# Routing in three groups of batches, with nine expert tiles run inside the first part

## What is computed

```python
x = x + xattn(_layernorm(x), fside, ctx)    # per batch: smooth_quant_linear, silu(gate) * up, smooth_quant_linear
t = _layernorm(x)
scores = einsum('btd,de->bte', t, router_w)                  # 8 experts
w, idx = top_k(softmax(scores), 2); w = w / sum(w)
y = sum over the two chosen e of  w_e * ((silu(t @ gate_proj[e]) * (t @ up_proj[e])) @ down_proj[e])
x = x + y
```

## Time and profile before

| | |
|---|---|
| median of 3 runs | 421.02 us (420.9 to 422.14) |
| the profiled execution | 421.27 us, span 419.4 us |
| PE, DVE, ACT, POOL busy | 77%, 50%, 50%, 59% of the span |
| first part | 0 to about 196 us |
| routing, to the first gather | about 196 to 220 us |
| 39 tiles, from the first expert matmul | 226 us to the end |

### The profile page before, as it was taken

The page is one execution under the profiler, slowest core; times in us unless marked ns, Lnnn a source line. Parts: engine busy times, 40 slices in busy tenths (PEclk is TensorE's granted clock), DMA queues, the critical chain, the costliest instruction groups (busy, mean ns, idle before and its releaser), DMA issues.

```text
span 419.4 us, 5809 instructions
## 1 busy us (share of the span) xinstructions
PE 322.5 (77%) x1712; PEld 202.4 (48%) x1738; DVE 209.2 (50%) x442; ACT 209.7 (50%) x378; POOL 246.4 (59%) x260
## 2 busy tenths in 40 slices
PE   0638758879887678861166999999999999999960
PEld 0525445567656446651143555555555555555530
DVE  2584899887898855500871333333333333323310
ACT  1558559878779767453101444444444444444430
POOL 2484698677869565458304265666566656656440
PEclk9957966995899795865555999999999999999996
DMA  7936406693178347035004266766666666675552
GB/s 258 314 115 216 161 41 203 192 358 100 26 253 325 109 144 275 27 125 225 1 0 127 36 117 102 131 112 115 120 125 106 116 110 125 106 134 102 90 70 27
DMA packets 26667, 57.00 MB, mean 136 GB/s; under 512 B 2576, under 2 KB 12816, under 8 KB 24592
## 3 DMA queue, kind: packets, MB, share of 16 engines
q0 software_dynamic: 8816, 20.71, 27.5%
q1 hardware_dynamic: 17824, 35.93, 24.6%
HBM read 37.50 MB, written 19.14 MB: 135 GB/s over the span
## 4 chain that ended last, share of the span: by engine, by line
issue 27%; POOL 12%; PE 8%; POOLq 2%; DMA 1%; ACT 0%; DVE 0%; SPq 0%
POOL xg L772 8%; PE bank_r L1007 4%; PE bank_h L1029 3%; POOLq L778 2%; POOL out L782 1%; DMA xg<-tokens,gather_at 1%; POOL hold_p L198 1%; POOL number L754 1%; PE bank_t L995 1%; PE bank_q L1018 0%; POOL out L757 0%; ACT y L953 0%; DVE aT L900 0%; ACT aT L948 0%; POOL no_later L764 0%
## 5 line engine op out<-in xcount | busy, mean ns | idle before, releaser
L1007 PE MATMUL bank_r<-gu_hi,xT 128*128 x312 | 107.0, 385 | 1.0 <-DVE xT L891 0.2
L782 POOL DMA_INDIRECT out<-y,scatter_at x39 | 61.7, 1583 | 51.2 <-ACT y L953 50.0
L891 DVE SCALAR_TENSOR_TENSOR xT<-bank_t,xT 128x512 f16<-128x512 f32 x39 | 27.0, 691 | 66.3 <-ACT xT L933 66.3
L772 POOL DMA_INDIRECT xg<-tokens,gather_at x39 | 38.5, 986 | 29.1 <-DVE gather_at L881 17.3
L1007 PE MATMUL bank_r<-gu_lo,xT 128*128 x144 | 55.1, 383 | 0.0
L1029 PE MATMUL bank_h<-dn_hi,aT 128*128 x156 | 52.8, 379 | 1.7 <-DVE aT L900 1.4
L953 ACT ACTIVATE y<-bank_h,slot_weight 128x512 f32<-128x512 f32 x39 | 26.8, 687 | 36.8 <-PE bank_h L1029 36.8
L1007 PEld LDWEIGHTS bank_r<-gu_hi,xT 128*128 128x128 f16 x312 | 30.8, 99 | 29.5 <-issue 2.5
L360 POOL TENSOR_TENSOR gu_lo<-stage,gu_hi 128x1024 bf16<-128x1024 f32 x16 | 34.0, 2129 | 13.1 <-ACT gu_hi L578 13.0
L933 ACT ACTIVATE xT<-bank_t 128x512 f16<-128x512 f32 x39 | 23.0, 589 | 24.8 <-PE bank_t L995 24.7
L906 DVE SCALAR_TENSOR_TENSOR gated<-bank_r,gated 128x256 f32<-128x256 f32 x39 | 16.6, 425 | 37.3 <-ACT gated L941 37.3
(11 more groups left out here) (156 smaller groups left out, 629.7 us busy)
## 6 DMA issues: line engine op xcount, KB each, us to landing
x_in<-in_x SPq DMA_DIRECT2D x4, 1024.0 KB, 5.4
w_in<-in_fside_BxS2xS SPq DMA_DIRECT2D x4, 1024.0 KB, 6.3
stage<-in_L_ffn_gate_proj SPq DMA_DIRECT2D x8, 512.0 KB, 4.9
stage<-in_L_ffn_up_proj SPq DMA_DIRECT2D x8, 512.0 KB, 3.7
stage<-in_L_ffn_down_proj SPq DMA_DIRECT2D x8, 512.0 KB, 4.8
x<-in_x SPq DMA_DIRECT2D x4, 1024.0 KB, 6.2
out<-x SPq DMA_DIRECT2D x4, 1024.0 KB, 6.7
tokens<-xn SPq DMA_DIRECT2D x4, 1024.0 KB, 6.4
```

The costliest lines, as they stand in the source:

```text
L772: pool.indirect_dma_start(out=xg[:, i % XG], out_offset=None, in_=tokens_dram, in_offset=bass.IndirectOffsetOnAxis(ap=gather_at[:, i:i + 1 ...
L782: pool.indirect_dma_start(out=out, out_offset=bass.IndirectOffsetOnAxis(ap=scatter_at[:, i:i + 1], axis=0), in_=y[:, i], in_offset=None, c ...
L891: dve.scalar_tensor_tensor(out=xT[i % 2][:, 1].rearrange("p c t -> p (c t)"), in0=bank_x[:, i % 2], scalar=X_SCALE, in1=xT[i % 2][:, 0].re ...
L1007: ins = pe.matmul(bank_gu[:, i % 2], xT[i % 2][:, part, c], rhs[:, cols], start=(c == 0 and n == 0), stop=(c == C - 1 and n == 2))
```

## The change

What it does:

- The batches are routed in three groups, (0, 1), (2) and (3). An expert has 16 fixed slots of 128 rows. "choose g" finds the two experts of each row, "place g" the slot and lane, with a one-hot over slots and one over lanes for each batch and choice; "table g" adds the sorted rows to a table; "list" and "indices" take the filled slots out of it as tiles.
- After group 0 the first nine (`EARLY`) full tiles are listed, gathered and run as phase 0, woven into the orders of the first part; the other 30 follow as phase 1, when group 2 is placed. There is no second block.
- The router multiplies x1, the rows ahead of the second layer norm, with weights whose column mean is taken off (`rwc`). The weights of the two choices come from the difference of their scores times `rstd`, by Tanh ("weigh g"); the softmax goes.
- The early tiles use buffers of the first part: xg and y are three rows each in the staging buffer, so all 24 pieces must be split before the first gather. `y` of the late tiles is a ring of eight.
- An early scatter waits for the landing of the one before it. ACT's "take y i" of an early tile waits until scatter i - 3 has landed.
- "x scales" and "w1 scales" make the scale of all four row groups at once, and all orders are new.
- At the start, SP waits for a memset on POOL and stores the padding rows before it loads x.

```diff
+EARLY = 9
-    "load x 0, load w1 0, load expert 0, load expert 1, load expert 2, load w2 0, load x 1, load expert 3, "
+    "load x 0, load w1 0, load expert 0, load w2 0, load expert 1, load x 1, load expert 2, load expert 3, "
...
+    GROUPS = [(0, 1), (2,), (3,)]
+    PHASES = ([(0, 0, EARLY, GROUPS[0])] if EARLY else []) + [(len(GROUPS) - 1, EARLY, MOST, range(B))]
...
+        ahead = pool_order.index(("gather", EARLY)) + 1
+        pool_order[ahead:ahead] = [("gather", EARLY + n) for n in range(1, J)]
+        act_order.append(("x high", EARLY))
+        dve_order.append(("x low", EARLY))
+        for i in range(EARLY, TILES):
+            if i + J < TILES:
+                pool_order.append(("gather", i + J))
+            pool_order.append(("scatter", i))
...
+            sp.wait_ge(sem("zeroed"), 1)
+            sp.dma_start(tokens_dram[N:N + P], blank).then_inc(sem("pad_stored"), 16)
...
+            def gather(i):
+                phase = phase_of[i]
+                if phase not in started:
+                    started.append(phase)
+                    pool.wait_ge(sem("pad_stored"), 16)
+                    pool.wait_ge(sem("lo_done"), 3 * E)
+                    for b in PHASES[phase][3]:
+                        pool.wait_ge(sem(f"tokens_stored{b}"), 16)
+                    pool.wait_ge(sem("gather_ready"), phase + 1)
+                before = before_in(3, J, i)
+                if before is not None:
+                    ring_t.done(pool, "x low", 0, before)
...
+            def scatter(i):
...
+                if i < EARLY:
+                    if i > 0:
+                        pool.wait_ge(sem("added"), 16 * i)
+                    landing = sem("added")
+                else:
+                    before = pool.value_load(scatter_after[0:1, i:i + 1], min_val=1, max_val=MOST)
+                    pool.wait_ge(sem("landed"), before)
...
+                for n, b in enumerate(GROUPS[g]):
+                    for k in range(K):
...
+                        for s in range(2):
+                            then(dve.tensor_tensor(onehot[:, k, s], number[:], spread(place_of[:, s, n, k], [P, P, J], 1), ALU.is_equal))
...
+                        if step > 0:
+                            after_sort(step - 1)
+                        dve.tensor_tensor(packed[:], spread(onehot[:, k, 0], [P, 3, P, J], 1), spread(values[:, :, b, k], [P, 3, P, J], 2),
+                                          ALU.mult).then_inc(sem("packed"), 1)
...
+            def take_y(i):
...
+                before = before_in(3, 2 * J, i)
+                if before is not None:
+                    if i < EARLY:
+                        act.wait_ge(sem("added"), 16 * (before + 1))
+                    else:
+                        act.wait_ge(sem("landed"), before - EARLY + 2)
```

More of the change, by code:

```diff
@@ new lines, in block_kernel @@
+        ring_w = Ring(pe_order, [bank_r[:, 1]], sem("w_row_filled"), sem("w_row_taken"),
+                      {"rows 1": 1, "rows 2": 1, "w1 scale row": 1, "table": 1, "indices": 1}, [("a low", 1)])
+        ring_q = Ring(pe_order, banks(bank_q), sem("q_filled"), sem("q_taken"),
+                      {"x transposed": C, "w1 transposed": C, "a transposed": IC, "w2 transposed": IC,
+                       "tokens": 2, "scores": 1, "take y": 1})
+        ring_h = Ring(pe_order, banks(bank_h), sem("h_filled"), sem("h_taken"), {"product 1": J, "product 2": J, "up first": 1})
@@ L517, in _ @@
+            in_turn(dve_order,
+                    {"choose": choose, "place": place, "table": add_to_table, "list": list_tiles, **({"done": tiles_done} if EARLY else {}),
+                     "indices": indices, "x low": x_low, "up": up, "a low": a_low,
+                     "moments 1": partial(moments, 0, x_in, sem("x_in"), 1), "moments 2": partial(moments, 1, x1, sem("x1_ready"), J),
                      "w1 columns": partial(weight_columns, "w1 columns", 0), "w2 columns": partial(weight_columns, "w2 columns", 1),
@@ L584, in silu, with take_tokens @@
                     act.activation(h[:, j:j + 2, 0:I], h[:, j:j + 2, 0:I], ACT.Silu).then_inc(sem("silu_done"), 1)
[L586 to L589 removed]
+            def take_tokens(pair):
                 for j in range(2):
[L591 to L592 removed]
@@ new lines, in sort @@
+            def sort(g):
+                bank = ring_w.fill(pe, "table", 0, g)
+                steps = K * len(GROUPS[g])
+                for n in range(steps):
+                    step = K * GROUPS[g][0] + n
+                    pe.wait_ge(sem("packed"), step + 1)
+                    for j in range(J):
+                        ins = pe.matmul(bank[:, 0:3 * P].rearrange("p (v l) -> p v l", v=3), onehot[:, n % K, 1, :, j], packed[:, :, :, j],
+                                        start=(n == 0 and j == 0), stop=(n == steps - 1 and j == J - 1))
+                    ins.then_inc(sem("sorted") if n < steps - 1 else ring_w.filled, 1)
@@ L689, in _ @@
                      "product 2": partial(product, "product 2", aqT, dqT, ("a transposed", "w2 transposed")),
-                     "tokens A": partial(tokens, 0), "tokens B": partial(tokens, 1),
-                     "scores A": partial(router, 0), "scores B": partial(router, 1)})
+                     "tokens": tokens, "scores": router,
+                     "place": rank, "table": sort, "indices": compact, "x low": transpose_x,
+                     "up first": partial(gate_up, 0), "up rest": partial(gate_up, 1), "a low": transpose_a, "take y": down})
```

834 lines of the change are left out of this document (463 added, 371 removed), and 83 rows, old and new, of tables (ACT_ORDER, DVE_ORDER, PE_ORDER, POOL_ORDER).

## The result

The changed kernel takes 426.31 us in the median of 4 runs (425.23 to 429.26), the kernel before 420.96 beside it (418.98 to 422.14); the ratio is 1.0131, with a 95% interval of 1.0099 to 1.0163. It is slower by 1.3%, a small loss, but its interval is clear of 1, where I had forecast 409.5 us. The profiled execution, the shortest of the four, took 425.23 us for a span of 423.3, so the sum of the prediction is judged against 425.2. All ratios here use executions in the chip's faster state; of the kernels traced, only that of e2 was caught in a slower execution.

What follows compares the result with a forecast made beforehand. Bounds: DVE with ACT in the first part, then the routing, then PE in the tiles. Gather 9 at 235.8 + 17.3 + 152.5 + 2.0 = 407.6 us span, plus 1.9 around it, 409.5; range 397 to 425.

Steps and rivals of the forecast that it cites:

- to product 2 3: Last batch, from product 1 3 to product 2 3 on DVE: 26.7 us without waits, plus waits, reaching 203.9.
- to gather 9: From product 2 3 to the first late gather: 24.7 us of DVE work plus 7.2 of waits, reaching 235.8.
- G to T: From gather 9's start (G) to tile 9's first matmul (T): 17.3 us, waiting for scatter 5's landing.
- T to the end: From tile 9's first matmul to the end: 152.5 us for 30 late tiles, plus 2.0 for late gathers.
- From x scales 3 to product 1 3: DVE in the last batch: 25.2 us of work plus 4.6 of waits, so product 1 3 begins at 166.9.
- The port: Rival: POOL stands still during DVE's one-hots and packed rows, 7 us on gather 9, 416.5 us; chance 0.05.
- 30 tiles x 4.54: Late tiles: each keeps the old spacing of 4.54 us, 152.5 us in all, if only PE bounds them.
- the 2.0 for gather 13 and 14: Late tiles: PE waits for gathers 13 and 14, held on POOL behind scatters 8 and 9; 2 us.
- The start: Load x 2.1 us late behind a memset and a transfer, offset by seven fewer small DVE instruction pairs.
- The two middle legs: Product 1 3 to product 2 3, then to gather 9: DVE work plus walked waits, ending at 203.9 and 235.8.
- the hold before tile 9: ACT's take y 8 waits for scatter 5's landing, delaying tile 9's x high; removing this alone gains little.
- PE's clock: Rival: early tiles run at 1.2 GHz, gather 9 16 us later, 425.5 us; chance 0.17.

Runs made afterwards that it cites:

- e2: Changed kernel with three added POOL tensor_tensor of 1024 elements beside place 1: 433.35 us, ratio 1.0257 to the kernel before.
- e1: Changed kernel with POOL's low pieces 20, 21 and 22 waiting for DVE's fourth packed row: 431.16 us, ratio 1.0214 to the kernel before.
- g2: Changed kernel without POOL's low pieces 18 to 22, so results lose those parts: 420.08 us, ratio 0.9939 to the kernel before.
- h1: Changed kernel with late tiles' expert register load moved ahead of the down matmuls on PE: 422.36 us, ratio 1.0035 to the kernel before.
- h2: Changed kernel with nine early result buffers, register load moved ahead of down matmuls, pad store behind first loads, POOL gathers further ahead: 411.07 us, ratio 0.9776.
- f3: Changed kernel with nine early result buffers, gathers ahead of scatters, DVE/POOL overlap reordered, pad store behind first five loads: 420.58 us, ratio 0.9968.
- e3: Changed kernel with nine result buffers for early tiles instead of three, scatter order kept: 428.99 us, ratio 1.0179 to the kernel before.
- f4: Changed kernel with EARLY = 0, all 39 tiles after the grouped routing: 446.62 us, ratio 1.0599 to the kernel before.
- f1: Changed kernel with low pieces 21 and 22 delayed, choose 0 and gap instructions moved, to keep DVE and POOL apart: 427.20 us, ratio 1.0122.

## Why the prediction was wrong

By its own steps, the last column in us:

| Step | Predicted | Measured | Difference |
|---|---|---|---|
| x scales 3 ends | 137.1 | 139.56 | +2.5 |
| to product 1 3 | 29.8 | 37.7 | +7.9 |
| to product 2 3 | 37.0 | 38.7 | +1.7 |
| to gather 9 | 31.9 | 32.3 | +0.4 |
| G to T | 17.3 | 17.1 | -0.2 |
| T to the end | 154.5 | 157.9 | +3.4 |

**The step that failed** is "From x scales 3 to product 1 3", through the part "The port", which the sum puts at nothing. I priced the one-hots and packed rows rightly (0.44 and 0.96 against 0.42 and 0.95), and named the contention, but let POOL stand for DVE, with POOL's slack to cover it. The trace shows the other direction, and e1, e2 and g2 confirm it: DVE's instructions wait for POOL's, and small ones that I had not counted wait as long as large ones. The held instructions lose 10.1 us; the rest of the leg was 2.2 shorter than I walked it. Taking away 6.3 us of these holds brings gather 9 forward by 7.2 us (g2). The rival came near this size by luck, with the wrong engine waiting; its own terms (7.6 less 3 of slack, and 3.8) also add up to 8.4 and not to 7. The Trainium skill does not leave the direction open (SBUF — State Buffer, "SBUF: two separate sides"): there the shared pair of ports goes to whichever starts first, a GpSimd instruction or a DVE instruction in a 2-port perf mode or with two SBUF inputs (these only against a GpSimd instruction that reads SBUF), for the whole of it, and the other waits. By that rule DVE waits wherever a 2.1 us piece has started ahead of a short DVE instruction with two SBUF inputs, and this trace agrees, with 1.92 us for an instruction on one element. I had read only the line in GPSIMD Engine Reference.

**The term mis-sized next** is "30 tiles x 4.54" in the span from T. I compared the matmuls of a tile and found them the same; the register load had moved to directly ahead of the x transposes. From T to the end the trace has 3.4 us more than the sum, in which the 2.0 for gather 13 and 14 is right (their two distances are 5.70 and 5.46), and h1 gives back 4.

**The start.** The load was late as reckoned (issued at 3.24, DVE from 8.31). I let seven pairs of small instructions outweigh it. The 2.5 us measured at x scales 3 can't be told from what the traces differ there, 138 to 143 at slot_row. With the pad store behind the first loads, h2 has slot_row at 137.19, ahead of all nine, but f3, with the same edit, ends x scales 3 at 140.46; the price of the start stays open.

**What held.** The two middle legs, with 13.9 us of waits walked, were right to 2.1 us in their sum; whether each wait was right was not looked at. Right were also the hold before tile 9, its cause, the place of the second, and that the first alone is worth little (e3). PE's clock, my only rival for a slower kernel, did not come about: the clock was 0.74 at 180 to 200 us and 1.00 in the next stretch. The breakeven, a gather 9 at 247.5, was passed by 0.8 us, and the late tiles did the rest: without the 7.2 us of the port and the 3.4 of the register load the sum is 414.6, inside the range.

**Where the expected gain went.** Nine tiles are 40.9 us of PE. f4 shows that the groups cost 14.6 at T, and the longer distance of the tiles 6, before any tile is early. The early tiles then put T from 240.57 to 265.35, 24.8 us, of which 10 are the hold before tile 9, and the second hold, for gather 13, follows. What is left in the medians is 20 us of gain against 25 of cost; in the traces, where f4's is its shortest execution, 17 against 21.

## What to carry to other kernels

When small dependent instructions go onto DVE, look first at what POOL runs in the same stretch. A DVE instruction that reads two sources in SBUF, and some with one, can cost up to one POOL instruction, however small it is. In e1 and f1 moving the one along the other only moved the holds; they shrank where POOL's work was taken away (g2). When a transfer waits on its queue for another's landing, everything behind it waits as well; a bigger buffer and a new order have to come together, and the hole then moves to the next place where a gather stands behind such a wait. Read the diff of the PE queue for instructions that do no matmul: moving one register load per tile from ahead of the transposes to ahead of the down matmuls gave back 1.0% here (h1).
